# A graph network on one Trainium2 core: descents and laying out in one block, tables by destination beside the sort by source, attention weights in the GCN stage's block

## The chip, the cores and the metric

The kernel is one launch on one NeuronCore of a Trainium2 chip. The metric is device time in microseconds, the median of several executions. A profile is one further execution, recorded instruction by instruction.

## The reference, cut to what matters

Four graph layers over 50,000 nodes of 128 features and 25,000 edges (`src`, `dst`, 16 edge attributes), each followed by a layer norm of `x + layer(x)`:

```
x = norm(x + sage(x, src, dst))                     # mean over incoming edges, one product
x = norm(x + gcn2(gcn1(x)))                         # sums by src, self loops, W1 and W2
x = norm(x + gatv2(x, src, dst, edge_attr_16))      # 4 heads; logits from Wl x[src] + Wr x[dst] + We attr
x = norm(x + gat2(relu(gat1(x))))                   # 2 heads each, self loops
```

Every sum over edges is a segment sum by `dst` or by `src`. In the inputs the edges already stand in the order of `dst`. The edges are padded to 25,088 = 128 partitions x 196, the nodes to 50,176.

## The kernel before, in words

Each stage is a `Phase` (line 69): it allocates tensors and semaphores, opens one block in which every engine has its own program, and on leaving clears its semaphores (L101) and makes all engines meet (L102). The block itself also ends in a meeting, for which each engine first drains (the line of the `with nc.Block()`). So nothing of a stage starts before all of the one before has ended. Engines order themselves inside a block by semaphores alone; each runs its program in the order written. DMAs are issued from SP and ACT (queues q1 and q10 of the page) and, the indirect ones, from POOL (q0).

The stages that the change touches, in order of time:

- `find_descents` (phase `fd`, L2543) loads `dst` as 128 x 196, counts places where the next key is smaller, and leaves the count in `descents`. `values_load` then reads it into registers and a branch is taken on it.
- If there is any descent, two sort passes `d1`, `d2` would run. There is none in these inputs, so `lay_out_sorted` (phase `lo`, L2576) runs: `load_edges` (L371) loads `dst` and `src`, and the attributes straight into columns 2 to 17 of a row of 18 words, which is 25,088 pieces of 64 bytes; POOL casts the two keys into columns 0 and 1; ACT stores all 1764 KB as `by_dst`.
- `sort_pass` `s2` (L220) sorts (src, dst) pairs by the high bits of `src` into `by_src`. DVE and PE make a histogram, then in 28 slots of 7 columns DVE makes one-hots and ranks and POOL scatters 128 rows of 8 bytes per column. There are four slots of buffers: SP passes on, per slot, that the scatters have landed (L162), and DVE waits for that before it overwrites a slot (L318). ACT does nothing in this block but free the slots at its start.
- `walk_tables` (L731) for `by_dst` (phase `dw`, with `krel_rows`), then for `by_src` (phase `sw`): SP loads the rows as 98 x 256; a linked chain on DVE with PE and ACT in between makes tables of steps; for `dw` four blocks of `krel` are turned on PE, copied by ACT and stored by SP.
- `walk` `e0`, `node_sage`, `walk` `e1a` and `e1b`, then `node_gcn` (phase `n1`, L1446): 98 blocks of 512 nodes, six in flight. SP loads w1, w2, then per block `ys` and `ag`; DVE mixes and makes sums, PE turns and multiplies, POOL makes the deviation, ACT moves, applies and issues the store.
- `edge_tables` (phase `et`, L420): SP loads `by_dst` as 128 x 196 rows (`et_pay`) and, one word a partition, the key after and the key before; ACT copies the attributes into `e.att`; DVE makes some 45 small linked results, with one product on PE.
- `gatv2_weights` (phase `g2w`, L1599): SP loads biases and matrices, DVE splits biases and `We` into bf16 parts in 17 linked steps, SP spreads them by 12 small DMAs into `g.edge` and `g.bl_parts`. Then `gatv2_logits` (phase `lg`) starts.

## Time and profile before

| | us |
|---|---|
| median of 3 executions | 5425.68 (5424.95 to 5432.66) |
| the profiled execution's own time | 5423.13 |
| its span | 5421.4 |
| phase `fd` and branch, up to the first load of `lo` | 4.57 to 10.76 |
| phase `lo`, up to the first load of `s2` | 10.76 to 38.66 |
| phase `s2`, up to the load of `dw` | 38.66 to 354.63 |
| phase `dw`, up to the load of `sw` | 354.63 to 381.80 |
| phase `n1`, from the load of w1 to the last store's issue | 1487.37 to 1772.57 |
| phase `et`, up to the first load of `g2w` | 1775.90 to 1798.98 |
| phase `g2w`, up to the first load of `lg` | 1798.98 to 1820.61 |

Starts and ends are those of the profile's timeline, counted from the start of the span. Busy shares over the whole span are 65% for PE, 62% for DVE, 41% for ACT and 67% for POOL.

### The profile page before, as it was taken

What the parts mean: (1) busy time and instruction counts of PE and PEld (TensorE: products, weight loads), DVE (VectorE), ACT (ScalarE), POOL (GpSimd) and SP (SyncE); (2) the same over time, 40 slices, a digit from 0 to 9 for tenths busy, and PEclk for the clock granted to TensorE, in tenths of its full rate; (3) what the DMA queues carried; (4) which work ended last, traced back from release to release, by engine and by line L of the source; (5) the groups of instructions that cost most, each with busy time, mean ns of one, the idle gap of its engine ahead of it and who ended that gap; (6) DMA issues with size and microseconds to landing.
All of it is one profiled execution on the core that took longest, in us unless ns stands there. A gap on an engine that the chain in (4) does not pass through costs nothing. (4 is left out here: it accounts for less than half of the span.)

```text
span 5421.4 us, 98328 instructions
## 1 busy us (share of the span) xinstructions
PE 3522.2 (65%) x21061; PEld 2447.6 (45%) x21062; DVE 3343.9 (62%) x13740; ACT 2223.5 (41%) x6490; POOL 3610.6 (67%) x4923
## 2 busy tenths in 40 slices
PE   4527699777788499969689999620009995100398
PEld 3417688676766244422166666420007774100133
DVE  6535488444488477678578888632508886153288
ACT  0005477676667244423278888400004441000155
POOL 2747577777645477727578888775765556757698
PEclk8659999999999799979899999855559997555699
DMA  1005488888899532101134444351119885311498
GB/s 30 1 20 159 150 275 274 240 257 251 239 278 287 198 106 52 52 14 38 34 130 141 141 141 141 109 136 36 41 64 291 292 289 164 89 32 41 149 342 300
DMA packets 550968, 816.27 MB, mean 151 GB/s; under 512 B 118566, under 2 KB 267629, under 8 KB 550466
## 3 DMA queue, kind: packets, MB, share of 16 engines
q1 hardware_dynamic: 396820, 559.50, 32.9%
q0 software_dynamic: 69184, 122.90, 9.2%
q10 hardware_dynamic: 84816, 132.30, 6.5%
q8 instruction: 44, 0.72, 0.1%
q14 instruction: 104, 0.85, 0.1%
HBM read 493.48 MB, written 329.46 MB: 152 GB/s over the span
## 5 line engine op out<-in xcount | busy, mean ns | idle before, releaser
L620 POOL DMA_INDIRECT agg_dst<-e_rows,e_put_i x392 | 390.3, 996 | 203.7 <-issue 118.8
L1868 POOL DMA_INDIRECT e_rows<-h,e_other_i x392 | 389.0, 992 | 148.5 <-issue 118.9
L1209 POOL TENSOR_TENSOR n_rstd<-n_rstd,minus_half 128x4 f32<-128x4 f32 x294 | 334.9, 1139 | 23.1
L689 POOL DMA_INDIRECT agg<-e_msg,e_put_i x196 | 194.4, 992 | 164.4 <-DVEq L718 113.2
L1222 ACT ACTIVATE n_o<-n_y_ps,n_shift,n_rstd 128x128 f32<-128x128 f32 x784 | 293.6, 458 | 11.9 <-POOL n_shift L1489 11.5
L364 POOL DMA_INDIRECT by_src<-s_pay_s,s_place_i x196 | 188.4, 961 | 113.9 <-issue 58.8
L2367 POOL TENSOR_TENSOR n_u<-n_u 128x512 f32<-128x512 f32 x98 | 124.5, 1270 | 205.3 <-DVE n_u L2314 205.3
L895 POOL DMA_INDIRECT x_rows<-x,d_other_i x196 | 185.9, 948 | 112.7 <-issue 58.8
L1690 POOL DMA_INDIRECT lg_rows<-x,e_other_i x196 | 186.0, 949 | 109.8 <-issue 59.4
L2168 PE MATMUL n_y_ps<-n_w,n_gt 128*128 128x128 f32 x1568 | 239.1, 275 | 0.0
L937 PE MATMUL e1b_bank<-y_rows,e1b_hot 128*128 x1584 | 196.4, 281 | 62.0 <-ACT e1b_bank L1049 41.3
L895 POOL DMA_INDIRECT y_rows<-m,s_other_i x196 | 186.4, 951 | 74.9 <-issue 54.6
L937 PE MATMUL e1a_bank<-y_rows,e1a_hot 128*128 x1584 | 196.5, 281 | 60.9 <-ACT e1a_bank L1035 32.5
L937 PE MATMUL e_bank<-x_rows,e_hot 128*128 x1584 | 198.7, 283 | 56.9 <-ACT e_bank L1007 41.6
L1769 DVE TENSOR_TENSOR lg_z<-lg_z_ps,lg_z 128x512 f32<-128x512 f32 x196 | 135.2, 690 | 162.5 <-ACT lg_z L1735 162.5
L1103 PE MATMUL e_xl_ps<-gat_wl,e_xg 128*128 128x512 f32 x392 | 223.1, 651 | 18.0 <-ACT e_xg L1076 18.0
L895 POOL DMA_INDIRECT y_rows<-y,s_other_i x196 | 185.7, 948 | 65.4 <-issue 55.8
L1690 POOL DMA_INDIRECT lg_rows<-x,e_key_i x196 | 186.6, 952 | 59.7 <-issue 59.7
L937 PEld LDWEIGHTS e1b_bank<-y_rows,e1b_hot 128*128 128x128 f32 x1584 | 184.2, 194 | 74.3 <-issue 74.3
L937 PEld LDWEIGHTS e_bank<-x_rows,e_hot 128*128 128x128 f32 x1584 | 186.3, 193 | 69.5 <-issue 69.5
L937 PEld LDWEIGHTS e1a_bank<-y_rows,e1a_hot 128*128 128x128 f32 x1584 | 184.4, 194 | 73.3 <-issue 73.3
L1222 ACT ACTIVATE n_x3s<-n_r,n_shift,n_rstd 128x128 f32<-128x128 f32 x392 | 161.6, 482 | 131.3 <-POOL n_shift L1213 131.3
(510 smaller groups left out, 11760.1 us busy)
## 6 DMA issues: line engine op xcount, KB each, us to landing
n_ag<-agg_dst SPq DMA_DIRECT2D x294, 264.0 KB, 3.9
n_hs<-h SPq DMA_DIRECT2D x196, 264.0 KB, 3.9
n_xs<-x SPq DMA_DIRECT2D x196, 256.0 KB, 4.0
agg_dst<-e_ev SPq DMA_DIRECT2D x196, 132.0 KB
y<-n_o ACTq DMA_DIRECT2D x98, 264.0 KB, 3.5
e1a_fed<-y SPq DMA_DIRECT2D x196, 132.0 KB
m<-e1a_ev SPq DMA_DIRECT2D x196, 132.0 KB
e1b_fed<-m SPq DMA_DIRECT2D x196, 132.0 KB
```

What stands on the lines that cost most here:

```text
L364: pool.indirect_dma_start(out=target, out_offset=bass.IndirectOffsetOnAxis(ap=place_i[:, s, k:k + 1], axis=0), in_=pay_s[:, s, k, :], in_o ...
L620: pool.indirect_dma_start(out=agg, out_offset=bass.IndirectOffsetOnAxis(ap=e.put_i[:, c:c + 1], axis=0), in_=rows[:, c, :], in_offset=None ...
L689: pool.indirect_dma_start(out=agg, out_offset=bass.IndirectOffsetOnAxis(ap=e.put_i[:, c:c + 1], axis=0), in_=msg[:, g % SLOTS, k, 0:out_wi ...
L895: pool.indirect_dma_start(out=rows[:, c, 0:fetched], out_offset=None, in_=table, in_offset=bass.IndirectOffsetOnAxis(ap=e.other_i[:, c:c + ...
L937: ins = pe.matmul(bank[:, bass.ds(to + h * width, summed)], hot[:, s, k, h * P:(h + 1) * P], flat_rows[:, bass.ds(row, summed)], start=Fal ...
L1103: pe.matmul(self.xl_ps[k][:, :], xg[:, s % 2, k, :], self.wl[:, :], start=True, stop=False)
L1209: st(pool.tensor_tensor(rstd, rstd, keep.minus_half[:, :], ALU.pow))
L1222: ins = act.activation(out[:, g, 0:D], r[:, g, :], ACT.Identity, bias=shift[:, g:g + 1], scale=rstd[:, g:g + 1])
L1690: pool.indirect_dma_start(out=rows[:, g % SLOTS, k, i, :], out_offset=None, in_=x, in_offset=bass.IndirectOffsetOnAxis(ap=of[:, c:c + 1], ...
L1769: dve.tensor_tensor(z[:, c % 2, :], z_ps[c % 2][:, :], z[:, c % 2, :], ALU.max).then_inc(z_out, 1)
L1868: pool.indirect_dma_start(out=rows[:, c, :], out_offset=None, in_=h, in_offset=bass.IndirectOffsetOnAxis(ap=e.other_i[:, c:c + 1], axis=0))\
L2168: ins = pe.matmul(y_ps[s % BANKS][:, g, :], gt[:, s % 2, j, g, :], w2[:, j, :], start=False, stop=(g, j) == (GB - 1, 1), skip_group_check= ...
```

## The change

Five edits, none of which alters what is computed:

1. `find_descents` and `lay_out_sorted` become one block. SP loads `dst`, then the attributes as one contiguous tensor `raw`, then `src`, then the first key of the next partition. POOL casts the keys, ACT copies `raw` into the rows' columns 2 to 17 and stores them. The branch comes after it and has no else part.
2. `walk_tables` for `by_dst` and `edge_tables` now return functions that write their engines' programs into the block of `sort_pass` `s2`, behind the sort's own. All their loads, and the four stores of `krel`, are issued from ACT, the walk's first; PE's part waits until all 196 ranks are made (`ranked` at J + 4). The PSUM tensors of the sort become one of eight banks, which the tables share. Their two phases are closed behind that of the sort, each with its clearing and meeting.
3. `e.att` is no longer copied by ACT from `et_pay`; a DMA loads it from columns 2 to 17 of `by_dst`.
4. The loads of `gatv2_weights` and that DMA are issued by SP at the start of the block of `node_gcn`, ahead of w1 and w2.
5. DVE's splitting and SP's spreading of `gatv2_weights` stand behind `node_gcn`'s own programs in its block (`rest`).

```diff
-def sort_pass(nc, keep, name, words, digits, high, load, target):
+def sort_pass(nc, keep, name, words, digits, high, load, target, beside=None):
...
-        hist_ps = ph.ps("hist_ps", [P, 512])
-        total_ps = ph.ps("total_ps", [P, 512])
-        before_ps = ph.ps("before_ps", [P, 512])
-        run_ps = [ph.ps(f"run_ps{q}", [P, 512]) for q in range(4)]
+        banks = ph.ps("banks", [P, 8, 512])
+        hist_ps, total_ps, before_ps = (banks[:, i, :] for i in range(3))
...
             n_loads = load(block, ph, pay, loaded)
+            more = ph.stack.enter_context(ExitStack())
...
+            if beside is not None:
+                with nc.allow_non_contiguous_dma(reason="one word of an edge's payload"):
+                    beside(block, more, banks, lambda pe: pe.wait_ge(ranked, J + 4))
...
-def edge_tables(nc, keep, name, rows, words, stack, full, att_stack):
+def edge_tables(nc, keep, name, rows, words, stack, full):
...
-        e.att = att_stack.enter_context(nc.sbuf_tensor(f"{name}_att", [P, J, ATT_IN], F32))
-    with Phase(nc, name + "t") as ph:
+    def lay_out(block, more, banks):
+        ph = more.enter_context(Phase(nc, name + "t"))
...
+        spread = banks[:, 0, 0:2 * P].rearrange("p (t q) -> p t q", t=2)
...
+        @block.scalar
+        def _(act):
+            act.dma_start(pay[:, :, :], view).then_inc(loaded, 16)
+            act.wait_ge(preset, 2)
+            act.dma_start(after[0:P - 1, :], view[1:P, 0, 0:1]).then_inc(loaded, 16)
+            act.dma_start(before[1:P, :], view[0:P - 1, J - 1, 0:1]).then_inc(loaded, 16)
+        @block.vector
+        def _(dve):
+            link = linked(dve, chain)
+            dve.memset(after[:, :], -1.0).then_inc(preset, 1)
...
+    return e, lay_out
...
-    with Phase(nc, name + "w") as ph:
+    def lay_out(ph, block, banks, banks_free):
...
+        begun_ps, opened_ps, high_ps, low_ps = (banks[:, i, :] for i in range(4))
+        other_ps = banks[:, 4, :].rearrange("p (h t) -> p h t", h=2)
...
+        def load(engine):
+            engine.dma_start(pay[:, :, :], rows.rearrange("(q r) w -> q r w", q=EQ)).then_inc(loaded, 16)
...
+        if krel_rows is None:
+            block.sync(load)
+        else:
+            block.scalar(load)
+        @block.scalar
+        def _(act):
+            act.wait_ge(turned, 1)
+            act.activation(e.other_i[:, :].rearrange("p (q h) -> p h q", h=2), other_ps[:, :, 0:EQ], ACT.Copy)
+            if krel_rows is not None:
+                act.wait_ge(step_turned, 1)
+                for b, (_, n) in enumerate(STEP_BLOCKS):
+                    act.activation(e.chunk_hot[0:n, b, :, :], step_ps[0:n, b, 0:2 * EQ].rearrange("p (h q) -> p h q", h=2), ACT.Copy)
+                act.wait_ge(krel_turned, 1)
+                for b, (_, n) in enumerate(STEP_BLOCKS):
+                    act.activation(krel_b[0:n, b, :], krel_ps[0:n, b, :], ACT.Copy).then_inc(krel_copied, 1)
+                for b, (first, n) in enumerate(STEP_BLOCKS):
+                    act.wait_ge(krel_copied, b + 1)
+                    act.dma_start(krel_rows[first:first + n, :], krel_b[0:n, b, :]).then_inc(krel_out, 16)
+                act.wait_ge(krel_out, 16 * len(STEP_BLOCKS))
...
+        @block.tensor
+        def _(pe):
+            banks_free(pe)
+            pe.wait_ge(loaded, 16)
...
+    if krel_rows is not None:
+        return e, lambda block, more, banks, banks_free: lay_out(more.enter_context(Phase(nc, name + "w")), block, banks, banks_free)
+    with Phase(nc, name + "w") as ph:
+        banks = ph.ps("banks", [P, 8, 512])
...
-def node_gcn(nc, keep, y1, agg, w, beta, x2):
+def node_gcn(nc, keep, y1, agg, w, beta, x2, beside):
...
+        more = ph.stack.enter_context(ExitStack())
         with nc.Block() as block:
+            rest = beside(block, more)
...
+            rest()
...
-def gatv2_weights(nc, keep, stack, w):
+def gatv2_weights(nc, keep, stack, w, edges, att):
...
-    with Phase(nc, "g2w") as ph:
+    def lay_out(block, more):
+        ph = more.enter_context(Phase(nc, "g2w"))
...
+        @block.sync
+        def _(sp):
+            sp.dma_start(both[0:1, 0, :], w["bl"].unsqueeze(0)).then_inc(loaded, 16)
+            sp.dma_start(both[0:1, 1, :], w["br"].unsqueeze(0)).then_inc(loaded, 16)
+            sp.dma_start(we[:, :], w["We"]).then_inc(loaded, 16)
+            sp.dma_start(conv[:, :], w["conv_bias"].unsqueeze(0)).then_inc(loaded, 16)
+            sp.dma_start(g.wl[:, :], w["Wl"]).then_inc(edge_in, 16)
+            sp.dma_start(g.wr[:, :], w["Wr"]).then_inc(edge_in, 16)
+            sp.dma_start(g.att[:, :], w["att"].rearrange("h d -> (h d)").partition_broadcast(P)).then_inc(edge_in, 16)
+            sp.dma_start(att[:, :, :], edges.rearrange("(p j) w -> p j w", p=P)[:, :, 2:WD]).then_inc(edge_in, 16)
+        def rest():
             @block.sync
...
-                sp.wait_ge(edge_in, 48)
+                sp.wait_ge(edge_in, 64)
...
+        return rest
+    return g, lay_out
...
-def find_descents(nc, keep, dst, descents):
+def lay_out_sorted(nc, keep, src, dst, attr, target, descents):
...
+        pay, raw, ends = ph.sb("pay", [P, J, WD]), ph.sb("raw", [P, J, ATT_IN]), ph.sb("ends", [P, J], I32)
+        attr_in, ends_in, laid, stored = (ph.sem(n) for n in ("attr_in", "ends_in", "laid", "stored"))
...
                 sp.dma_start(key[:, :], view).then_inc(loaded, 16)
+                sp.dma_start(raw[:, :, :], attr.rearrange("(p j) a -> p j a", p=P)).then_inc(attr_in, 16)
+                sp.dma_start(ends[:, :], src.rearrange("(p j) -> p j", p=P)).then_inc(ends_in, 16)
                 sp.wait_ge(preset, 1)
                 sp.dma_start(after_i[0:P - 1, :], view[1:P, 0:1]).then_inc(loaded, 16)
...
-def lay_out_sorted(nc, src, dst, attr, target):
-    with Phase(nc, "lo") as ph:
-        pay = ph.sb("pay", [P, J, WD])
-        loaded, stored = ph.sem("loaded"), ph.sem("stored")
-        with nc.Block() as block:
-            n_loads = load_edges(nc, src, dst, attr)(block, ph, pay, loaded)
+            @block.gpsimd
+            def _(pool):
+                pool.wait_ge(loaded, 32)
+                pool.wait_ge(ends_in, 16)
+                pool.tensor_copy(pay[:, :, 0], key[:, :]).then_inc(laid, 1)
+                pool.tensor_copy(pay[:, :, 1], ends[:, :]).then_inc(laid, 1)
             @block.scalar
             def _(act):
-                act.wait_ge(loaded, n_loads)
+                act.wait_ge(attr_in, 16)
+                act.activation(pay[:, :, 2:WD], raw[:, :, :], ACT.Copy).then_inc(laid, 1)
+                act.wait_ge(laid, 3)
                 act.dma_start(target.rearrange("(p j) w -> p j w", p=P), pay[:, :, :]).then_inc(stored, 16)
                 act.wait_ge(stored, 16)
...
-        find_descents(nc, keep, dst, descents)
+        lay_out_sorted(nc, keep, src, dst, attr, by_dst[1], descents)
         unsorted = nc.values_load(descents[0:1, 0:1], min_val=0, max_val=EPAD)
         with nc.If(unsorted > 0):
             sort_pass(nc, keep, "d1", WD, LOW, False, load_edges(nc, src, dst, attr), by_dst[0])
             sort_pass(nc, keep, "d2", WD, HIGH, True, load_sorted(by_dst[0]), by_dst[1])
-        with nc.Else():
-            lay_out_sorted(nc, src, dst, attr, by_dst[1])
-        sort_pass(nc, keep, "s2", WS, HIGH, True, load_edges(nc, src, dst, None), by_src)
+        to_dst, lay_out_edges = edge_tables(nc, keep, "e", by_dst[1], WD, stack, True)
         with ExitStack() as walk_stack:
-            on_dst = walk_tables(nc, keep, "d", by_dst[1], WD, walk_stack, stack, krel_rows)
+            on_dst, lay_out_walk = walk_tables(nc, keep, "d", by_dst[1], WD, walk_stack, stack, krel_rows)
+            def tables_on_dst(block, more, banks, banks_free):
+                lay_out_walk(block, more, banks, banks_free)
+                lay_out_edges(block, more, banks)
+            sort_pass(nc, keep, "s2", WS, HIGH, True, load_edges(nc, src, dst, None), by_src, tables_on_dst)
             on_src = walk_tables(nc, keep, "s", by_src, WS, walk_stack)
             with nc.sbuf_tensor("x_rows", [P, J, ROW], F32) as rows:
                 walk(nc, keep, "e0", on_dst, rows, x, ROW, agg_dst, FromZero(ROW))
...
             with nc.sbuf_tensor("y_rows", [P, J, ROW], F32) as rows:
                 walk(nc, keep, "e1a", on_src, rows, y1, D, m1, FromRows(y1))
                 walk(nc, keep, "e1b", on_src, rows, m1, D, z2, FromScaledRows(m1))
-            node_gcn(nc, keep, y1, z2, (gcn["W1"], gcn["W2"]), GCN_BETA, x2)
         with ExitStack() as att_stack:
-            to_dst = edge_tables(nc, keep, "e", by_dst[1], WD, stack, True, att_stack)
-            gatv2_edges(nc, keep, to_dst, gat2, x2, agg2)
+            to_dst.att = att_stack.enter_context(nc.sbuf_tensor("edge_att", [P, J, ATT_IN], F32))
+            g, lay_out_weights = gatv2_weights(nc, keep, att_stack, gat2, by_dst[1], to_dst.att)
+            node_gcn(nc, keep, y1, z2, (gcn["W1"], gcn["W2"]), GCN_BETA, x2, lay_out_weights)
+            gatv2_edges(nc, keep, to_dst, g, gat2, x2, agg2)
         node_gatv2(nc, keep, x2, agg2, gat2, gat[0], x3, h3, a3)
         gat_edges(nc, keep, "e3", to_dst, on_dst, krel_rows, h3, a3, a_edges, agg_dst)
         node_gat(nc, keep, x3, h3, agg_dst, gat[0], gat[1], s4, h4, a4)
...
```

The bodies left out for DVE, PE and ACT are those of before, line for line.

## Rows read from the trace of the kernel before

**Rows 1.** Timeline, first 40 us: start, duration, engine, line, what [idle before <-releaser].

```profile
4.57 0.39 SPq L2554 DMA_DIRECT2D fd_key<-dst  x1
...
8.69 0.16 DVE L2568 CAST descents<-fd_total_ps 128x1 int32<-128x1 f32 x1 [0.68 <-PE fd_total_ps L2573]
...
10.76 0.37 SPq L382 DMA_DIRECT2D lo_ends<-dst  x1
...
11.64 0.72 SPq L384 DMA_DIRECT2D lo_pay<-edge_attr  x1
...
32.20 0.35 ACTq L2587 DMA_DIRECT2D by_dst<-lo_pay  x1
38.66 0.34 SPq L382 DMA_DIRECT2D s_ends<-src  x1
```

**Rows 2.** DMA view, 11.6 to 32.2 us: traffic while `lo_pay` is loaded.

```profile
DMA packets 1875, 1.85 MB, mean 90 GB/s; under 512 B 48, under 2 KB 1872, under 8 KB 1872
```

**Rows 3.** Timeline, 1766 to 1799 us: end of `n1`, the edge tables.

```profile
1769.19 0.16 DVE L1578 SCALAR_TENSOR_TENSOR n_mv<-n_ys,n_mv 128x4 f32<-128x4 f32 x1
...
1772.57 0.34 ACTq L1536 DMA_DIRECT2D x<-n_o  x1
1775.90 0.33 SPq L457 DMA_DIRECT2D et_pay<-by_dst  x1
...
1776.80 5.31 SPq L460 DMA_DIRECT2D et_before<-by_dst  x1
1783.97 2.82 ACT L466 ACTIVATE e_att<-et_pay 128x3136 f32<-128x3136 f32 x1 [11.44 <-DMA et_before<-by_dst]
...
1797.45 0.15 DVE L516 TENSOR_SCALAR e_split<-et_whole 128x1 f32<-128x1 f32 x1
```

**Rows 4.** The scatter of the sort by line: count, ns min/median/max, first and last start.

```profile
L364 POOL DMA_INDIRECT by_src<-s_pay_s,s_place_i x196: 954/958/1293, 96.1 to 343.0; - x196
```

**Rows 5.** The one-hot writes of the sort beside that scatter, same columns.

```profile
L285 DVE TENSOR_SCALAR s_onehot<-iota_h,s_digs x196: 253/265/476, 87.7 to 302.7; 128x196 f16<-128x196 f16 x196
```

**Rows 6.** Queue instructions of the sort's block (L251), 344 to 356 us, same columns.

```profile
L251 POOLq DRAIN  x1: 8151/8151/8151, 345.7 to 345.7; - x1
```

**Rows 7.** Timeline, 303 to 412 us: last rank, and the tables by destination.

```profile
310.08 0.17 DVE L321 COPY s_pay_s<-s_pay 128x14 f32 x1
...
354.63 0.39 SPq L772 DMA_DIRECT2D dw_pay<-by_dst  x1
...
364.40 0.40 DVE L795 CAST dw_key_i<-dw_pay 98x256 int32<-98x256 f32 x1 [54.15 <-DMA dw_pay<-by_dst]
...
375.58 0.57 DVE L833 SCALAR_TENSOR_TENSOR d_krel<-dw_tile_off,dw_low_ps 128x396 f32<-128x396 f32 x1
...
378.17 1.74 SPq L776 DMA_DIRECT2D krel_rows<-dw_krel_b  x4
381.80 0.34 SPq L772 DMA_DIRECT2D sw_pay<-by_src  x1
```

**Rows 8.** Queue instructions of one phase's exit (L101), 1817 to 1821 us.

```profile
L101 POOLq DRAIN  x1: 58/58/58, 1820.2 to 1820.2; - x1
```

**Rows 9.** Timeline, 1798 to 1823 us: the attention weights.

```profile
1798.98 0.23 SPq L1618 DMA_DIRECT2D g2w_both<-L_gnn_bl  x1
...
1801.30 0.68 DVE L1640 TENSOR_TENSOR g2w_both<-g2w_both 1x512 f32<-1x512 f32 x1 [3.69 <-DMA g2w_conv<-L_gnn_conv_bias]
...
1811.10 3.73 SPq L1628 DMA_DIRECT2D gat_edge<-g2w_we_part  x6
...
1820.61 1.76 SPq L1676 DMA_DIRECT2D lg_no_edges<-L_gnn_conv_bias  x4
```

**Rows 10.** Timeline, start of `n1`: first weights.

```profile
1487.37 0.96 SPq L1469 DMA_DIRECT2D n_w<-L_gnn_W  x2
...
1489.70 0.23 DVE L1547 TENSOR_SCALAR n_near<-ident 128x128 f32<-128x128 f32 x1 [12.55 <-DMA n_w<-L_gnn_W]
```

**Rows 11.** Windows view, steady part of `n1`: busy us by engine, clock, DMA share, GB/s.

```profile
1512.00:1745.00 233.00, 203.74 (x1179) 146.02 (x1178) 205.13 (x1090) 172.02 (x421) 122.76 (x252) 1.00 0.95 286
```

More of the change, by code:

```diff
@@ L237, in sort_pass @@
         base = ph.sb("base", [P, digits])
[L238 to L241 removed]
+        banks = ph.ps("banks", [P, 8, 512])
+        hist_ps, total_ps, before_ps = (banks[:, i, :] for i in range(3))
+        run_ps = [banks[:, 3 + q, :] for q in range(4)]
         loaded, digit_ready = ph.sem("loaded"), ph.sem("digit_ready")
@@ L525, in spread_ends @@
+        @block.tensor
+        def _(pe):
+            pe.wait_ge(diag_ready, 2)
+            pe.matmul(spread[:, :, :], keep.ones[:, :], diag[:, :, :], start=True, stop=True).then_inc(spread_done, 1)
+    return e, lay_out
 def spread_ends(pe, keep, heads, diag, spread_ps, diag_ready, spread_done, n):
@@ L863, in walk_tables @@
+    if krel_rows is not None:
+        return e, lambda block, more, banks, banks_free: lay_out(more.enter_context(Phase(nc, name + "w")), block, banks, banks_free)
+    with Phase(nc, name + "w") as ph:
+        banks = ph.ps("banks", [P, 8, 512])
+        with nc.Block() as block:
+            lay_out(ph, block, banks, lambda pe: None)
     return e
```

280 lines of the change are left out of this document (113 added, 167 removed).

## The prediction

> **What bounds the kernel now.** I read the views in this order. The page's chain of waits names almost nothing before the last stage (its shares are all 0%), so it can't price this change. The kernel is a row of stages with a meeting of all engines between them, and each stage has its own bound; what the change is worth is read from the timeline at the places where one stage hands over to the next. The reader is to see there a small set of intervals in which nearly all engines idle: 4.57 to 38.66 us before the sort by source can start [rows 1], 354.63 to 381.80 for the tables by destination [rows 7], 1775.90 to 1798.98 for the edge tables [rows 3], and 1798.98 to 1820.61 for the attention weights [rows 9]. Each is a load's latency and then a linked chain. The two stages that are to take this work in are bound otherwise. The sort's second half runs at POOL's pace: 196 scatters start from 96.1 to 343.0 us, 1.266 us apart, of which 0.958 is the instruction [rows 4]. DVE is done with its last slot at 310.25 [rows 7], and after the last scatter POOL drains for 8.15 us, from 345.7 to 353.9 [rows 6]. So DVE, PE and ACT are free for 43 us there. The GCN stage has no such room: the DMA engines are 0.95 busy at 286 GB/s, and PE and DVE are busy 204 and 205 of 233 us [rows 11]. What is put in front of it or behind it comes on top.
>
> **Part 1, descents and laying out together.** Before, the way from the first load to the sort's first load is 38.66 - 4.57 = 34.1 us. 20.6 of them (11.64 to 32.20) are the attribute load in 64-byte pieces, which keeps the DMA engines at 90 GB/s [rows 1, 2]. After, the same 1568 KB come as 128 long runs. The nearest row is `et_pay`, 1764 KB in long runs, landed with two tiny loads behind it 8.1 us after its issue (1775.90 to 1783.97) [rows 3]; scaled by size 7.2, behind a first issue of 0.45: landed at 4.57 + 0.45 + 7.2 = 12.2. ACT's copy into the rows is new here; the same size takes 2.82 in `e_att` [rows 3], so the store is issued at 15.1. POOL's two casts and DVE's count wait for the one-word load behind `raw`, which should land about 13, and end before ACT's copy does; if it lands 2 late, the store is up to 1 late. From the store's issue to the next stage's load is 6.5 [rows 1]. The branch, which stood ahead, now comes behind: 8.85 to 10.76 holds a stage's exit and the branch, 1.9 [rows 1], of which the exit is already in the 6.5, so 1.1. The sort's first load is then at 22.7: a gain of **16.0**. Bounds: 12 (the load as slow as the 9.8 of `dw_pay` [rows 7], the late word, two more for the branch) to 18.
>
> **Part 2, `dw_pay` in the sort's block.** ACT issues its 1764 KB at the moment when SP issues the two key loads for which the whole sort waits; before, these had the DMA engines alone. The trace has no small load beside a large one from another queue. From below the cost is 0. From above, the keys land when the large load does: it needs 9.8 [rows 7], a small one 2.3 [rows 10], so 7.5. I take the middle, **+4**: both queues get turns, but the large runs are long. Nothing else of the block waits for `dw_pay`.
>
> By the Trainium skill (DMA: Bandwidth & Descriptors, Queues, rings and completion order) each DMA engine takes turns between queues, one whole packet at a time; by that rule the keys get through before the large load ends, but each of their packets waits for one of its. That speaks for the middle too.
>
> **Part 3, the tables in the sort's cover.** DVE starts the walk's chain at 310.25; before it took 364.40 to 376.15, 11.75 [rows 7], so it ends at 322.0. PE's turn and ACT's copies took 2.0 more (378.17) and the stores of `krel` up to 2.75 with landing (1.74 issuing): 326.8. Only then does ACT issue `et_pay`, behind whose wait nothing else stands on ACT; 8.1 [rows 3] make 334.9. DVE's edge chain took 1783.97 to 1797.60, 13.6 [rows 3]: 348.5. The block ends at 353.9 by POOL's drain [rows 6], so 5.4 us are left, and both tables cost nothing. If the drain weren't there the block would end near 348.5, by DVE. What stays are two exits (clear and meet), about 0.4 to 0.6 each: in the exit of `g2w` it is 1820.2 to 1820.6 [rows 8, 9]. Gone is 381.80 - 354.63 = 27.2. Net **-26.2**, bounds -27 to -20 (the latter if the chain outlasts the drain by 6 us). The edge tables' 23.1 us are counted with part 5.
>
> The rule that speaks against this: by the Trainium skill (SBUF — State Buffer, SBUF: two separate sides, the "DVE blocks DMA" trap) a DVE copy in a two-port mode locks GpSimd out while it makes descriptors for its DMAs. The trace does not show it here: the 168 scatters issued while DVE wrote one-hots of 0.265 us [rows 5] and the 28 alone after 310 have one median of 958 ns with a minimum of 954 [rows 4]. As a mechanism of this kernel it is the third rival.
>
> **Part 4, loads ahead of the GCN stage.** SP now issues eight loads before w1 and w2, on the same queue. Four are tiny, about 0.3 each to issue: 1.2. Three are 256 KB, 0.79 MB at the 286 GB/s of [rows 11]: 2.7. The eighth is `e.att` straight from `by_dst`: 25,088 pieces of 64 bytes again, now every 72 bytes on the DRAM side. The nearest row is the load that part 1 gets rid of: 20.6 from issue to use, less 2.3 of latency [rows 1, 10], so 18.3. DMAs of one queue start in order, so w1, w2 and the first `ys` and `ag` stand behind all this; w1 landed 2.3 after its issue before [rows 10], and lands 1.2 + 2.7 + 18.3 = 22.2 later now. DVE's first mix needs it, and at a DMA share of 0.95 [rows 11] the stage never catches up. **+22**. Bounds: from below, pieces at the rate of long runs (1568 KB in 5 us) and the loads partly beside each other, +7; from above, twice the time a piece, +40. I take the row of equal pieces, since what differs is only the side on which they are strided.
>
> By the Trainium skill (DMA: Bandwidth & Descriptors, How a descriptor splits into AXI transactions) a read that doesn't start at a multiple of 256 bytes is begun at the boundary below. Of such reads the 72-byte step gives slightly longer ones than the 64-byte step, an estimate from that page of some 10%; the sum would be 2 us higher.
>
> **Part 5, edge tables and weights after the GCN stage.** DVE's last sum ends at 1769.35 [rows 3]. Then stand the 17 split steps, 1801.30 to 1811.10, 9.8, and from SP's first small store to the next stage's first issue 1820.61 - 1811.10 = 9.5 [rows 9]. GCN's own last store is issued at 1772.57 [rows 3] and is covered. With 0.9 for the exit of GCN's own stage behind this (its last store to `et_pay` is 3.3, less about 2.4 of landing), `lg` begins at 1769.35 + 9.8 + 9.5 + 0.9 = 1789.5, where it was 1820.61: **-31.1** for the edge tables and the weights together (23.1 + 21.6 removed, 13.6 left as a tail). SP waits for the split with nothing queued behind it but these stores. Bounds -33 to -27.
>
> **Sum.** -16.0 + 4 - 26.2 + 22 - 31.1 = -47.3 on the profiled execution's 5423.1: 5375.8. The median shown is 2.5 above that execution, so I forecast **5378 us**.
>
> **Rivals.**
> 1. *The pieces are cheaper than in `lo`.* Reading strided DRAM into contiguous SBUF could run near the rate of long runs. For it: nothing in the rows but the other direction of the stride. Then part 4 is +7 to +9: 5364.
> 2. *They cost twice as much.* For it: the reads straddle more. Against it: the same count and size as in [rows 2]. +18: 5397.
> 3. *The tables' chain costs POOL.* If each DVE step of the two chains (25.4 us in all) held up descriptor writing for half of its time, the scatters, and with them the drain and the block's end, come 12 later: 5390. Against it [rows 4, 5]. The same size results if the chain outlives the drain.
> 4. *Slower than before.* One mechanism: the 64-byte reads ahead of w1 are paid singly. It decides from 47.3 + 18.3 = 65.6 us for them, 3.6 times the row. The price, from a row: SP held the issue of one load of 127 single words for 5.31 us [rows 3], 42 ns a word, and 1568 pieces on each of 16 engines at 42 ns are 65.6 us, just no change; at four times the row, 73 us, the kernel takes 5433. Against it: the load in [rows 2] moves a piece each 11.7 ns an engine, and those 5.31 us were spent behind 1764 KB still moving, which explains them.
> 5. *The change doesn't do what it says*, as when ACT's issue of `dw_pay` or `raw` blocks its queue so that the store of `by_dst` is late: a few us only, inside the range and counted with the forecast.
>
> **How the numbers follow.** Forecast 0.60, with a range of its own from 5368 to 5388; rival 1, 0.12; rival 2, 0.13; rival 3, 0.08; rival 4, 0.04; the rest, 0.03, near no change. Within 0.2% means within 11 us of 5425.7, about what a measurement of this kernel can tell from no change. So faster 0.92 (all but rival 4 and the rest), same 0.04, slower 0.04. The range, 5358 to 5402, takes in rivals 1 to 3 and the bounds of part 2.
>
> **What would show each step.** The first load of the sort near 23 us, with `raw` landed by 12 (part 1); the sort's key cast 2.4 us after the load's issue if part 2 is 0, near 10 if it is all; DVE's `e_split` about 5 us before POOL's drain ends, and scatters of 958 ns beside it (part 3); the DMA engines at 90 GB/s for some 18 us at the start of `n1`, and w1 in use 24 us after the block's first issue instead of 2.3 (part 4); a tail of 14 us with SP's small stores alone (part 5). The prediction is wrong if the piece load takes under 10 or over 30 us, if the drain of POOL grows or goes, or if the sort's ranks are slowed by what shares its block.

## The result, and the profile after

The changed kernel took **5382.76 us** (median of 4 runs, 5378.64 to 5391.18) against 5428.80 for the kernel before beside it (4 runs, 5424.95 to 5432.66): ratio **0.9917**, 95% interval 0.99 to 0.9934. The forecast was 5378, the range 5358 to 5402. The profiled execution is the longest of the four (5391.18, span 5389.4), so the stretches below add up to -32 against the profiled execution before, not to -46; the difference is in the last row, where no instruction was changed.

| stretch | before | after | change | forecast |
|---|---|---|---|---|
| start to the sort's first load | 38.66 | 22.35 | -16.3 | -16.0 |
| to the sort's key cast | 3.39 | 11.85 | +8.5 | +4 |
| to `sw_pay` | 339.75 | 315.07 | -24.7 | -26.2 |
| to the first issue of `n1` | 1105.57 | 1103.25 | -2.3 | 0 |
| to `n_near` | 2.33 | 25.03 | +22.7 | +22 |
| to the last `n_mv` | 279.49 | 281.94 | +2.5 | 0 |
| to the first issue of `lg` | 51.42 | 20.58 | -30.8 | -31.1 |
| to the end of the span | 3600.8 | 3609.3 | +8.5 | 0 |

Each row is the difference of two starts in the timelines, before and after. The last stretch scatters from execution to execution: it was 3601.5, 3604.2, 3606.7 and 3608.1 us in four of the experiments' profiles (e8, e11, e10, e12), none of which changes anything there.

Timeline of the changed kernel, 20 to 36 us; answers to [rows 1].

```profile
22.33 0.60 ACTq L770 DMA_DIRECT2D dw_pay<-by_dst  x1
22.35 0.37 SPq L387 DMA_DIRECT2D s_ends<-src  x1
...
25.95 2.35 DVE L270 MEMSET s_onehot<- 128x2744 uint32 x1 [0.52 <-issue]
...
33.51 0.36 POOL L394 CAST s_pay<-s_ends 128x196 f32<-128x196 int32 x1 [19.87 <-DMA s_ends<-dst]
...
34.20 0.26 DVE L274 CAST s_key_i<-s_pay 128x196 int32<-128x196 f32 x1 [5.91 <-POOL s_pay L395]
```

Two things are late here. DVE clears the one-hots until 28.30, and the key cast could not have come before that. And POOL's cast waits until 33.51 for the second key load, 10.7 us after its issue. The DMA view of 22 to 34 us gives, by queue, packets, MB and share, and for the two key loads the time from issue to landing:

```profile
q10 hardware_dynamic: 112, 1.81, 53.9%
q1 hardware_dynamic: 288, 0.20, 7.5%
...
s_ends<-src SPq DMA_DIRECT2D x1, 98.0 KB, 9.6
s_ends<-dst SPq DMA_DIRECT2D x1, 98.0 KB, 10.7
```

The large load is 112 packets, the two small ones are 288. Both moved at once: by 30.5 us 95 of the 112 and 117 of the 288 had started (the same view, cut there). The small loads have the fewer bytes but the more packets, and they land when the large one is through.

Timeline of the changed kernel, 300 to 350 us, then its scatter by line and the queue instructions of the block (count, ns min/median/max, first and last start); they answer to [rows 4, 6, 7].

```profile
314.59 0.57 DVE L835 SCALAR_TENSOR_TENSOR d_krel<-dw_tile_off,s_banks 128x396 f32<-128x396 f32 x1
...
319.65 0.33 ACTq L462 DMA_DIRECT2D et_pay<-by_dst  x1
...
328.10 0.34 DVE L477 COPY et_key<-et_pay 128x196 f32<-128x196 f32 x1 [11.84 <-DMA et_before<-by_dst]
...
342.05 0.15 DVE L515 TENSOR_SCALAR e_split<-et_whole 128x1 f32<-128x1 f32 x1
...
349.27 0.39 SPq L770 DMA_DIRECT2D sw_pay<-by_src  x1
```

```profile
L365 POOL DMA_INDIRECT by_src<-s_pay_s,s_place_i x196: 954/958/1282, 88.7 to 336.4; - x196
...
L251 POOLq DRAIN  x1: 8061/8061/8061, 338.7 to 338.7; - x1
```

Both chains lie where they were put. The scatters keep their median of 958 ns, POOL's drain is 8.06 us and ends at 346.8, and DVE was done at 342.2: 4.6 us of cover left (forecast 5.4). From the drain's end to `sw_pay` it is 2.5 us (before, to `dw_pay`: 0.8); three phases are left there one after another. Three scatters beside the walk's chain are longer than their neighbours, 1.13, 1.08 and 1.28 us (at 310.3, 311.7 and 313.1).

Timeline of the changed kernel at the start of `n1`, and the DMA view of 1455.8 to 1476.5 us; they answer to [rows 2, 10].

```profile
1452.52 0.28 SPq L1634 DMA_DIRECT2D g2w_both<-L_gnn_bl  x1
...
1455.15 0.66 SPq L1641 DMA_DIRECT2D edge_att<-by_dst  x1
1455.86 19.78 SPq L1482 DMA_DIRECT2D n_w<-L_gnn_W  x2
...
1477.55 0.23 DVE L1560 TENSOR_SCALAR n_near<-ident 128x128 f32<-128x128 f32 x1 [35.28 <-DMA n_w<-L_gnn_W]
```

```profile
DMA packets 25617, 2.25 MB, mean 109 GB/s; under 512 B 25164, under 2 KB 25347, under 8 KB 25617
```

SP sits in the issue of w1 and w2 for 19.78 us, because the pieces stand ahead on its queue; the slices of that view settle at 86 to 88 GB/s, the 90 GB/s of [rows 2], though the view of [rows 2] counted 1872 packets and this one over 25,000.

Timeline of the changed kernel, end of `n1`; answers to [rows 3, 9].

```profile
1759.49 0.16 DVE L1591 SCALAR_TENSOR_TENSOR n_mv<-n_ys,n_mv 128x4 f32<-128x4 f32 x1
1759.57 0.67 DVE L1660 TENSOR_TENSOR g2w_both<-g2w_both 1x512 f32<-1x512 f32 x1
...
1769.37 3.74 SPq L1648 DMA_DIRECT2D gat_edge<-g2w_we_part  x6
...
1780.07 1.76 SPq L1698 DMA_DIRECT2D lg_no_edges<-L_gnn_conv_bias  x4
```

The tail is the split (9.8), twelve small stores (7.5) and landing and exits (3.2): 20.6 in all.

### The profile page after: what moved, and what is told of

It is laid out like the page before. It is cut to its first block and busy times, and to the rows that moved or that the text cites. A ratio compares the mean times of both kernels' runs of the same rounds, so it can differ in the third digit from the quotient of the medians.

```text
span 5389.4 us, 98297 instructions
## 1 busy us (share of the span) xinstructions
PE 3527.9 (65%) x21061; PEld 2451.3 (45%) x21062; DVE 3341.7 (62%) x13740; ACT 2224.4 (41%) x6490; POOL 3612.4 (67%) x4923
## 5 line engine op out<-in xcount | busy, mean ns | idle before, releaser
L619 POOL DMA_INDIRECT agg_dst<-e_rows,e_put_i x392 | 390.6, 996 | 204.3 <-issue 118.8
L947 PE MATMUL e_bank<-x_rows,e_hot 128*128 x1584 | 198.1, 283 | 57.2 <-ACT e_bank L1017 41.8
```

Source lines behind the costliest of these rows:

```text
L619: pool.indirect_dma_start(out=agg, out_offset=bass.IndirectOffsetOnAxis(ap=e.put_i[:, c:c + 1], axis=0), in_=rows[:, c, :], in_offset=None ...
L947: ins = pe.matmul(bank[:, bass.ds(to + h * width, summed)], hot[:, s, k, h * P:(h + 1) * P], flat_rows[:, bass.ds(row, summed)], start=Fal ...
```

## The experiments

Three groups were run, each with the kernel before on the same chip. In the first (e1 to e4) TensorE was granted less clock than elsewhere (0.77 over the span instead of 0.845) and stood idle for longer, and every kernel took about 6700 us, so its times are compared only within it.

| | what | median us | ratio to before (95%) |
|---|---|---|---|
| e1 | changed kernel again | 6693.83 | 0.996 (0.9947 to 0.9974) |
| e2 | `dw_pay` issued after the key casts | 6690.7 | 0.9955 (0.9941 to 0.9969) |
| e3 | `dw_pay` on SP behind the key loads | 6697.45 | 0.9966 (0.9948 to 0.9984) |
| e4 | edge rows in long runs, same place | 6681.23 | 0.9945 (0.9927 to 0.9964) |
| e5 | edge chain longer by 64 steps | 5396.3 | 0.9936 (0.9919 to 0.9953) |
| e6 | both mends | 5357.02 | 0.9865 (0.9848 to 0.9881) |
| e7 | both, and the split in the sort | 5349.57 | 0.985 (0.9834 to 0.9866) |
| e8 | changed kernel again | 5384.55 | 0.9918 (0.9901 to 0.9934) |
| e9 | part 1 alone | 5412.77 | 0.997 (0.9959 to 0.998) |
| e10 | weights in a block of their own | 5382.44 | 0.9916 (0.9899 to 0.9932) |
| e11 | pieces behind SP's loop | 5368.74 | 0.9893 (0.9876 to 0.9909) |
| e12 | changed kernel again | 5387.39 | 0.9924 (0.9907 to 0.994) |

**e1, e8 and e12: the changed kernel as reference.**

> The changed kernel once more, as the reference of the other runs of this group. Both theories: a median near 5383 us, ratio to the kernel before 0.991 to 0.992; the sort's key cast 11.9 us after the issue of its key loads; the GCN stage's n_near 25 us after the block's first issue.

> The changed kernel as the reference of this group. Both theories: 0.991 of the kernel before where the sort runs at POOL's pace, 0.996 where TensorE's clock is lower, as in the group before; the difference is in the block of the sort, which DVE's chain then ends instead of POOL's drain.

> The changed kernel as the reference of this group: 0.991 to 0.992 of the kernel before where the sort runs at POOL's pace, n_near 25 us after the block's first issue, tail 20.6.

In the two later groups the ratio is as expected. In the first the gain is 27.6 us instead of 46.5 or 41.2. The timeline of e1 and the queue instructions of its block say where the rest went:

```profile
419.77 0.15 DVE L515 TENSOR_SCALAR e_split<-et_whole 128x1 f32<-128x1 f32 x1
...
422.66 0.39 SPq L770 DMA_DIRECT2D sw_pay<-by_src  x1
```

```profile
L251 POOLq DRAIN  x1: 8061/8061/8061, 393.0 to 393.0; - x1
```

There the last rank comes only 11 us ahead of the last scatter (`dw_pay`'s cast 379.8, last scatter 390.6), where it is 34 ahead in the changed kernel's own profile (302.8 and 336.4). The chains start late, and DVE's last step ends 18.9 us after POOL's drain (401.1). The cover on which part 3 rests is the lead of DVE over POOL; where that lead goes, about 19 us of the gain go. The gains differ by 13.6 and 18.9 us between the groups. The sizes agree, but the gain of the first group is uncertain by some 9 us either way, and the kernel before has no profile there.

The granted clock alone doesn't explain what is slow in this group. Page rows of the walk `e0`, e1 and then the changed kernel (busy us, mean ns of one, idle before):

```profile
L947 PE MATMUL e_bank<-x_rows,e_hot 128*128 x1584 | 223.2, 291 | 273.7 <-issue 230.1
```

```profile
L947 PE MATMUL e_bank<-x_rows,e_hot 128*128 x1584 | 198.1, 283 | 57.2 <-ACT e_bank L1017 41.8
```

A matmul lasts 291 ns instead of 283, but PE idles 273.7 us before them instead of 57.2, and in 230.1 of these it waited for nothing that the profile shows. In the sort POOL waits 109.3 us in all for DVE's ranks (e1, 90 to 380 us), in the changed kernel 0.6 (90 to 300 us). So the lower clock comes with pauses of PE; which of them is the cause of the other, and what is behind both, no run here shows.

**e2 and e3: when and where `dw_pay` is issued.** e2:

```diff
+                @block.scalar
+                def _(act):
+                    act.wait_ge(loaded, n_loads)   # ahead of beside(...)
```

> ACT issues dw_pay only when the sort's two key loads have landed and been cast. Theory (the small loads stood behind the large one in the DMA engines, 9.6 and 10.7 us instead of 2.4): the key cast comes 3.4 us after the key loads' issue instead of 11.9, DVE's memset is not late, all of the sort moves 8.5 us earlier, and the kernel takes 8 to 9 us less than the changed one, about 5374. dw_pay then has 200 us of cover more than it needs. Rival (something else in the block's start is late, such as the branch or the engines' first instructions, whose idle time is booked as issue): the cast stays 8 us or more behind the loads' issue and the time doesn't move.

e3 moves it to SP's queue, behind the key loads and ahead of SP's loop:

```diff
-            block.scalar(load)
+            block.sync(load)
```

> dw_pay is issued by SP, on the queue of the key loads and behind them, instead of by ACT at the same moment. Theory (the packets of the two queues share the engines, and the large load, issued first, has its long runs ahead of the small ones): with the small loads ahead in one queue, they land after 2.5 to 3.5 us and the key cast is at most 4.5 us after their issue, nearly as early as with the late issue. Rival (the memory or the engines' write side is filled by the large load whatever the order): the cast comes 7 us or more after the issue, as in the changed kernel.

Timeline of e2, then of e3, 20 to 30 us:

```profile
22.00 0.37 SPq L391 DMA_DIRECT2D s_ends<-src  x1
...
25.42 0.36 POOL L398 CAST s_pay<-s_ends 128x196 f32<-128x196 int32 x1 [11.96 <-DMA s_ends<-dst]
...
26.26 0.58 ACTq L774 DMA_DIRECT2D dw_pay<-by_dst  x1
28.00 0.26 DVE L274 CAST s_key_i<-s_pay 128x196 int32<-128x196 f32 x1
```

```profile
22.24 0.38 SPq L387 DMA_DIRECT2D s_ends<-src  x1
...
23.13 1.39 SPq L770 DMA_DIRECT2D dw_pay<-by_dst  x1
...
25.71 0.36 POOL L394 CAST s_pay<-s_ends 128x196 f32<-128x196 int32 x1 [11.90 <-DMA s_ends<-dst]
...
28.18 0.26 DVE L270 CAST s_key_i<-s_pay 128x196 int32<-128x196 f32 x1
```

The small loads land in time in both: POOL casts 3.4 and 3.5 us after the first issue instead of 10.9 in e1. In e3 (landings after 2.2 and 3.0 us by its DMA view) the large load follows 0.5 us behind on the same queue and does no harm; the rival of e3, for which the order makes no difference, falls. e3 changes the order and the queue at once, and no run issues the large load 0.5 us later from ACT, so which of the two is the cure isn't separated. But the key cast comes 6.0 after the issue, not 3.4: it now waits for nothing but DVE's own clearing of the one-hots, and DVE starts in this block 2.7 us after SP. So the theory's 8.5 was too much by that. `sw_pay` comes 5.0 us earlier in both (417.7 against 422.7; in e4, whose sort is that of e1, it is 421.6); the medians (-3.1 and +3.6) are inside their scatter and don't tell.

**e9: part 1 alone.** The kernel before with the new `lay_out_sorted` and the old tables and weights.

> The kernel before with part 1 of the change alone: the descents and the rows by destination in one block, nothing else moved. Theory (the gain of part 1 is what the milestones show, 16.3 us to the first load of the sort): the sort's first load at 22.3 us, the key cast 3.4 after it as in the kernel before (nothing loads beside it), and the whole kernel 16 to 17 us faster than before, ratio 0.997. Rival (the sort's DVE starts late behind the branch, which now stands right ahead of it: its first memset came 2.7 us after the first load's issue in the changed kernel, and the key cast stands behind the clearing of the one-hots): the cast comes 6 us after the issue even with no load beside it, and the gain is 13 to 14 us.

Timeline of e9, 20 to 30 us:

```profile
22.36 0.37 SPq L382 DMA_DIRECT2D s_ends<-src  x1
...
26.03 2.35 DVE L269 MEMSET s_onehot<- 128x2744 uint32 x1 [0.52 <-issue]
...
28.49 0.26 DVE L273 CAST s_key_i<-s_pay 128x196 int32<-128x196 f32 x1
```

The rival is right in its place: with nothing loading beside the keys the cast is still 6.1 us after the issue (before: 3.4). Of the 8.5 us in the table 2.7 belong to part 1 (the branch now stands right ahead of the sort, and DVE's first instruction comes 2.8 us after SP's; why DVE is so late isn't shown) and 5.7 to part 2 (28.49 to 34.20). The cast is 13.6 us earlier than before; the medians say 15.9 less, ratio 0.997, which can't tell 13.6 from 16.

**e4, e11: the pieces.** e4 loads the rows whole at the same place, e11 moves the pieces behind SP's loop.

```diff
-            to_dst.att = att_stack.enter_context(nc.sbuf_tensor("edge_att", [P, J, ATT_IN], F32))
+            edge_rows = att_stack.enter_context(nc.sbuf_tensor("edge_rows", [P, J, WD], F32))
+            to_dst.att = edge_rows[:, :, 2:WD]
...
-            sp.dma_start(att[:, :, :], edges.rearrange("(p j) w -> p j w", p=P)[:, :, 2:WD]).then_inc(edge_in, 16)
+            sp.dma_start(att[:, :, :], edges.rearrange("(p j) w -> p j w", p=P)).then_inc(edge_in, 16)
```

> The edge rows for the attention are loaded whole at the same place, ahead of w1 and w2 (1764 KB in 128 long runs; the logits read their 16 words of each 18 in place), instead of 25,088 pieces of 64 bytes. Theory (the pieces are what holds up w1: 17 of its 22.7 us): n_near comes 11 to 13 us after the block's first issue (1.2 of issues, 2.7 for the 256 KB loads, 6 to 7 for the long runs, 2.3 of latency) instead of 25, the stage ends that much earlier, and the kernel takes 12 to 14 us less than the changed one. Rival (what costs is that eight loads and 2.5 MB stand ahead on one queue, in whatever pieces): n_near stays at 20 us or later and the gain is under 5 us. Strided reads in the logits may give up to 3 us back.

> The load of the edge rows in 25,088 pieces of 64 bytes stands behind SP's last load of the GCN stage instead of ahead of its first; all else as in the changed kernel. Theory: n_near 6 to 8 us after the block's first issue, as in the kernel with both mends (7.6), and the pieces, issued some 10 us before the last n_mv, take 20 us or more, hold SP and with it the twelve small stores: the tail grows from 20.6 to 25 to 33. Net 5 to 14 us less than the changed kernel, 5 to 12 more than with the long runs at the same place (but for the late dw_pay, 6 us of that difference). Rival (the pieces cost only where something waits on their queue for data, and behind the loop nothing does): the tail stays at 20.6 and all of the 17 us are gained.

Timeline of e4, start of `n1`:

```profile
2241.62 0.91 SPq L1482 DMA_DIRECT2D n_w<-L_gnn_W  x2
...
2251.23 0.23 DVE L1560 TENSOR_SCALAR n_near<-ident 128x128 f32<-128x128 f32 x1 [22.99 <-DMA n_w<-L_gnn_W]
```

e4: from the block's first issue (2238.50) to `n_near` it is 12.7 us, in e1 24.6 (2237.20 to 2261.8), and SP issues w1 and w2 in 0.91 us, where in e1 it is held for 19.28; the median is 12.6 less. As the theory said, and its rival (it's the queue's length in bytes) falls. e11, end of `n1`, 1715 to 1762 us:

```profile
1723.81 0.65 SPq L1645 DMA_DIRECT2D edge_att<-by_dst  x1
...
1738.86 0.16 DVE L1591 SCALAR_TENSOR_TENSOR n_mv<-n_ys,n_mv 128x4 f32<-128x4 f32 x1
...
1748.73 3.75 SPq L1648 DMA_DIRECT2D gat_edge<-g2w_we_part  x6
...
1759.45 2.03 SPq L1698 DMA_DIRECT2D lg_no_edges<-L_gnn_conv_bias  x4
```

Here my theory was wrong and the rival right. `n_near` comes after 6.9 us, and the tail is 20.6 as in the changed kernel: the pieces are issued 15 us ahead of the last `n_mv` (I had said 10) and are through when SP issues the first small store, 24.9 us later, at once (3.75 for six). All of the 18 us are gained: 5368.74 against 5387.39. Ahead of w1 the number of pieces costs, as e4 shows; behind the loop it costs nothing, as long as the pieces are through before the first store behind them is due. There they had 24.9 us, and where they stand ahead they hold SP for some 19.

**e10: is anything hidden in the shared block?** `lay_out_weights` in a block behind `node_gcn`:

```diff
-            node_gcn(nc, keep, y1, z2, (gcn["W1"], gcn["W2"]), GCN_BETA, x2, lay_out_weights)
+            node_gcn(nc, keep, y1, z2, (gcn["W1"], gcn["W2"]), GCN_BETA, x2, lambda block, more: lambda: None)
+            with ExitStack() as more:
+                with nc.Block() as block:
+                    lay_out_weights(block, more)()
```

> The changed kernel with the attention's weights and the edge rows' pieces taken out of the GCN stage's block and laid out in a block of their own behind it. Theory (in the shared block nothing of the loads was hidden: 22.7 us in front and a tail of 20.6): the GCN stage starts as before the change (n_near 2.3 us after the first issue), and behind it the pieces' 20 us run beside the split, with the small stores behind them on SP's queue, so 30 to 36 us from the last n_mv to the next stage. Together 7 to 13 us less than the changed kernel, though the work stands alone. Rival (the shared block did hide part of the loads beside GCN's first blocks): the time is the same as the changed one's or longer.

Timeline of e10, 1715 to 1776 us:

```profile
1736.60 0.16 DVE L1591 SCALAR_TENSOR_TENSOR n_mv<-n_ys,n_mv 128x4 f32<-128x4 f32 x1
...
1745.93 0.66 SPq L1641 DMA_DIRECT2D edge_att<-by_dst  x1
...
1755.43 13.29 SPq L1648 DMA_DIRECT2D gat_edge<-g2w_we_part  x6
...
1775.02 1.77 SPq L1698 DMA_DIRECT2D lg_no_edges<-L_gnn_conv_bias  x4
```

The stage starts as before the change (`n_near` 2.4 us after the first issue) and then 38.4 us stand between it and `lg`, more than the 30 to 36 expected, since SP sits in the small stores for 13.29 us behind the pieces. 38.4 against 22.7 + 20.6 = 43.3: 5 us less (expected 7 to 13), and the medians differ by 5.0 with intervals that overlap. So the size of the theory isn't shown; its direction rests on the stretches of one profile each. The rival (the shared block hides part of the loads) gets no support: laying the weights out in the GCN stage, at the place where the change does it, has no gain to show against a block of their own.

**e5: how much cover the drain gives.**

```diff
-                for h in range(HEADS):
+                for h in list(range(HEADS)) * 5:
                     dve.tensor_copy(e.cont_h[:, h, :], e.cont[:, :])
```

> The 16 head steps of the edge tables' chain are done five times instead of once, with the same results: 64 more DVE steps, four times the 3.6 us that they took in the profile of the changed kernel, so +14.4 us on DVE in the sort's block. Theory (these tables lie in the cover of POOL's drain, which ends 4.7 us after DVE's last step): with the scatters at POOL's pace as in the profiled execution, the first 4.7 us are free, sw_pay is issued 9.7 us later and the kernel takes about 10 us more than the changed one. Where TensorE's clock is lower and DVE's one-hot slots end with the last scatter, as in the group of runs before this, DVE ends the block already and the whole 14.4 are paid. Rival A (the DVE steps disturb POOL's descriptor writing, and the drain is long because of them): the scatters or the drain grow too, and more than 14.4 are paid. Rival B (the drain would wait in any case, as it begins only when the other engines are done): 14.4 are paid whatever the clock.

Timeline of e5, 336 to 358 us, and its block's queue instructions:

```profile
354.33 0.15 DVE L515 TENSOR_SCALAR e_split<-et_whole 128x1 f32<-128x1 f32 x1
...
357.23 0.39 SPq L770 DMA_DIRECT2D sw_pay<-by_src  x1
```

```profile
L251 POOLq DRAIN  x1: 8061/8061/8061, 338.0 to 338.0; - x1
```

The steps took 12.6 us, less than 14.4 (341.77 in e8 to 354.33). The drain starts and lasts as without them (338.0, 8.06; in e8 337.8), the last scatter starts at 335.5 in both, and `sw_pay` comes 8.9 us later (348.4 to 357.2): 12.6 less the 4.0 that DVE had left in e8 (its end 341.9, the drain's 345.9) are 8.6. Both rivals fall: the drain neither waits for DVE nor grows by its work, and the scatters take 247.7 us from first to last instead of 247.5. The medians differ by 11.8.

**e6 and e7: what the experiments point to.** e6 has e2's wait and e4's long runs at e11's place. e7 also takes the small weights out of `n1`: their loads are issued from ACT at the start of the sort's block, DVE splits them between the walk's chain and the edge chain, ACT stores them, and the three 256 KB loads go behind SP's loop.

```diff
+                split, rest = lay_out_small(block, more)   # the four small loads, from ACT
                 lay_out_walk(block, more, banks, banks_free)
+                split()
                 lay_out_edges(block, more, banks)
+                rest()                                     # the twelve small stores, from ACT
```

> Two mends of the changed kernel: dw_pay is issued when the key loads have been cast, and the edge rows for the attention are loaded whole (1764 KB in long runs) behind SP's last load of the GCN stage instead of ahead of its first. Theory: the sort starts 5 us earlier (measured with the late issue alone), w1 lands behind seven loads of which three are 256 KB, so n_near comes 6 to 7 us after the block's first issue instead of 25; the load behind SP's loop takes 8 us beside the last slots and the split and adds at most 2. Together 21 to 24 us less than the changed kernel. Rival (the DMA engines at a share of 0.9 decide the stage, so what is taken away in front is paid behind: 1764 KB are 6 us at 286 GB/s and the last blocks stand behind nothing): the last n_mv moves by less than 12 us, or the tail grows from 20.6 to over 28.

> As the kernel with both mends, and in addition the split of the attention's small weights (17 DVE steps, 12 small stores) is done in the sort's block, between the walk tables' chain and the edge tables' chain, where DVE waits 12 us for et_pay; the three 256 KB loads go behind SP's loop with the edge rows. Theory: the 9.4 us split fills a wait of DVE's and costs nothing there (where TensorE's clock is lower DVE waits there as well); of the GCN stage's tail of 20.6 us only the large loads' landing and the exits are left, 8 to 12 us; n_near comes 3 us after the block's first issue. So 8 to 12 us less than the kernel with both mends, 30 to 36 less than the changed one. Rival (the large loads at the end can't hide, 2.5 MB at 286 GB/s are 9 us and start when the last ag load is issued): the tail stays at 16 us or more and nothing is gained over the kernel with both mends but 3 us in front.

Timeline of e7: 308 to 346 us, start of `n1`, end of `n1`.

```profile
308.80 0.68 DVE L1646 TENSOR_TENSOR g2w_both<-g2w_both 1x512 f32<-1x512 f32 x1 [0.16 <-DVE d_krel L839]
...
318.61 0.42 DVE L1609 CAST g2w_we_part<-g2w_we_rest 16x512 bf16<-16x512 f32 x1
...
322.60 0.34 DVE L481 COPY et_key<-et_pay 128x196 f32<-128x196 f32 x1 [2.49 <-DMA et_before<-by_dst]
...
1450.85 0.23 DVE L1564 TENSOR_SCALAR n_near<-ident 128x128 f32<-128x128 f32 x1 [12.67 <-DMA n_w<-L_gnn_W]
...
1732.41 0.16 DVE L1595 SCALAR_TENSOR_TENSOR n_mv<-n_ys,n_mv 128x4 f32<-128x4 f32 x1
...
1739.97 1.28 SPq L1719 DMA_DIRECT2D lg_no_edges<-L_gnn_conv_bias  x3
```

e6: `n_near` 7.6 us after the first issue, tail 20.6, 27.5 us less than e8 (expected 21 to 24); its rival (the stage's DMA share takes it back) falls. e7: 7.5 less than e6 (expected 8 to 12) and **35.0 less than the changed kernel**, 81.5 less than the kernel before. The split fills DVE's wait for `et_pay`, which shrinks from 11.84 to 2.49 us; `n_near` comes 2.4 us after the first issue; the tail is 7.6 us, GCN's own last store and the exit. The 2.5 MB behind SP's loop cost nothing there, and its rival falls. The logits' strided reads of `edge_rows` cost nothing in their own stage: from its first load to the first instruction of the next stage it is 517.7 and 516.8 us in e6 and e7, and 516.9 to 517.4 in the eight profiles of the last two groups and of the main pair that read `e.att` or `edge_att`.

The medians place the gain of e7 over the changed kernel well, but not its split between the two steps. By the timelines `lg` starts at 1776.16 in e8, 1755.97 in e6 and 1739.97 in e7: 20.2 and then 16.0 us less, where the medians say 27.5 and 7.5. The rest of the span, unchanged, was 3601.5, 3612.1 and 3609.4 in these profiles, and e6's profiled execution is its slowest (5369.89, the other three 5356.42 to 5357.24). Nor is the split quite free in the sort: `sw_pay` comes 2.0 us later than in e6, and three scatters beside the split take 1.46 to 1.47 us. Neither kernel was run where DVE's lead is short, as in the first group.

## Why the prediction was right, step by step

**Part 1** said -16.0 to the sort's first load and it was -16.3, with `raw` in use at 11.96 (12.2) and the store issued at 14.85 (15.1). But the step ended too early: it counted the branch as 1.1 us of delay for SP and forgot that DVE, which has to clear the one-hots before it can cast the keys, comes out of it 2.7 us after SP. The gain at the key cast is 13.6 (e9), still inside the bounds of 12 to 18, and by 2.4 us the largest miss of the five.

**Part 2** said +4 from bounds 0 and 7.5, and measured 5.7. This term is too small by 1.7 us. The queues did get turns; what failed is the step from there to the middle. The DMA view of the kernel before counts 112 packets for `dw_pay` (354 to 365 us) and 288 for the two key loads (38 to 42 us). So by the rule that the prediction quotes, one whole packet at a time, the key loads outlast the large one: the rule speaks for the upper bound. The small loads landed 9.6 and 10.7 us after their issue, near the 9.8 of [rows 7] for the large one; only the 2.7 us by which DVE is late anyway kept the cost below the upper bound. e3 shows that the price goes when the key loads are issued first on the same queue.

**Part 3** said -26.2 with 5.4 us of cover left: -24.7 and 4.6. From the drain's end to `sw_pay` it was 2.5 us, 0.7 more than the step allowed for its two extra exits, and the scatters took 247.6 instead of 246.9 from first to last. So precise an account holds for this pair alone: from key cast to `sw_pay` the changed kernel took 311.9 to 315.5 us in five profiles (this one, e8, e10, e11, e12), the kernel with the old tables 339.75 and 337.6 (before, e9). Rival 3 is real, but small: in all eight profiles with the chain and a long lead of DVE the same three scatters take 1.08 to 1.29 us, and first to last is 247.5 to 248.9 instead of 246.9 (before, e9): at most 2 us and not 12. e5's 64 more DVE steps add 0.2 to e8's 247.5 and leave the drain as it is. The rival's last sentence, that the same loss results if the chain outlives the drain, is what e1 shows, and bigger than I made it (19 us, not 12). That the cover hangs on how fast the ranks come was not in the prediction.

**Part 4** said +22: +22.7. e11 parts it: the seven other loads cost 4.6 us (3.9 in the sum), and the pieces the 17.8 by which e12 is later (18.3). Its row, the equal pieces of [rows 2], was right within 0.5 us, and rivals 1, 2 and 4 fall with it. The 10% that the prediction estimated for reads off the 256-byte boundaries doesn't show (86 to 88 GB/s against 90). Nor does it follow from the rule as quoted: from the boundary below to the end of a piece it is 188 bytes on average with the 72-byte step and 160 with the 64-byte step, 18% more. That SP can't even issue what stands behind the pieces agrees with "the first `ys` and `ag` stand behind all this".

**Part 5** said -31.1: -30.8, with the tail of 20.6 in its three pieces (9.8 + 9.5 + 0.9 = 20.2 in the sum). The sign of "a tail of 14 us" counts from 1775.90, 6.5 us behind DVE's last sum, and is the same forecast.

**Sum.** By the table the changed stretches give -16.3 + 8.5 - 24.7 + 22.7 - 30.8 = -40.6, forecast -47.3; 5382.76 is 4.8 above 5378, and 46.0 below the kernel before. All five parts missed to the same side, as gains a little too large. The changed stretches of the profiled pair are at the low end: up to `lg` they and the rest give -40.5, in e8 and e12 -44.5 and -42.9 against the same profile before. The last, unchanged stretch moves by 8 us between executions, more than all errors of the forecast together (6.7): of the medians (-46.0, -46.5, -41.2) none can say whether -47.3 or -40.6 is nearer. That the median came within 5 us of the forecast is in part luck.

## To carry to other kernels

Price a load that is moved by what stands behind it: the same 25,088 pieces cost 17.8 us ahead of a stage's first load and nothing behind its last. Where loads share the DMA engines, count their packets and not only their bytes. Before work is put in another stage's cover, measure the cover at its place and ask what makes it: here it is one engine's lead over another, 4.0 to 4.6 us are left of it in five profiles with the changed kernel's sort, and 19 us are missing in e1. And an idle gap inside moved work (DVE's 11.8 us for `et_pay`) is itself a place for the next piece.

## What was new about the hardware

- Two small loads (98 KB each, 784 B a partition) issued on one queue 0.02 and 0.43 us after a load of 1764 KB on another landed after 9.6 and 10.7 us; with the second issued 0.5 us ahead of it on its queue they landed after 2.2 and 3.0 (e3). The large load was 112 packets, the small ones 288.
- A load of 64-byte pieces runs at 86 to 90 GB/s whether the view counts 1,872 packets or 25,600, and behind it SP is held in its next issues for 19.78 us (two loads) or 13.29 (six stores, e10), behind long runs for 0.91 (e4).
- POOL's drain at the end of the sort's block is 8,061 ns in the changed kernel and in all twelve experiments and 8,151 before; it doesn't wait for DVE and isn't lengthened by its work (e5).
- Linked DVE steps lengthen some of the scatters beside them: three to 1.08 to 1.29 us beside the walk's chain, and in e7 three more to 1.46 and 1.47 beside the split; the median is 0.96.
- In the first group, with a mean clock of 0.77 instead of 0.845, every kernel took some 1300 us more. 711 of them lie in the three walks of e1, which lasted twice as long as in the changed kernel's profile (first one-hots of `e0` to the last: 487 us against 246) at a granted clock of 0.72 against 0.98. The matmuls themselves were only 3% longer there (291 ns against 283); most of the time went into pauses of PE with no wait that the profile shows (230.1 us in `e0`). What caused the pauses and the lower clock stays open.
